# Attention and mixture-of-experts block on one core: new instruction orders for the first three steps and for the routed stage

## What is computed

```python
xn = layernorm(x)
# attention
c  = (xn @ W_to_kv.T) @ W_compress.T                  # 64 values a token
ch = layernorm(c) * gamma + beta
q, k, v = ch @ W_q.T, *split(ch @ W_kv.T)             # q and k get rotary tables
o  = softmax(causal(q @ k.T / 8)) @ v
attn = (o @ W_comp2lat.T) @ (W_to_kv + W_out_res.T) + b_out
# experts
logits = xn @ router_w.T                              # 16 experts, the 2 best are taken
shared = (silu(xn @ sh_gate) * (xn @ sh_up)) @ sh_down
routed = sum over the 2 best e of w_e * (silu(xn @ gate_e) * (xn @ up_e)) @ down_e
out = x + attn + shared + routed
```

## Time and profile before

| | us |
|---|---|
| median of 3 runs (lowest to highest) | 1816.95 (1816.46 to 1821.04) |
| the profiled execution, its own time | 1810.25 |
| its span | 1808.4 |
| PE busy in the span | 1729.9 (96%) |
| DVE, ACT, POOL busy | 1169.6, 751.4, 664.0 |
| prepare, routed, attend, by PE's first matmul of each | 0 to about 690, to 1484, to 1808 |

### The profile page before, as it was taken

The page is one execution under the profiler, slowest core; times in us unless marked ns, Lnnn a source line. Parts: engine busy times, 40 slices in busy tenths (PEclk is TensorE's granted clock), DMA queues, the critical chain, the costliest instruction groups (busy, mean ns, idle before and its releaser), DMA issues. The chain is left out here.

```text
span 1808.4 us, 27930 instructions
## 1 busy us (share of the span) xinstructions
PE 1729.9 (96%) x8349; PEld 1379.7 (76%) x8349; DVE 1169.6 (65%) x2284; ACT 751.4 (42%) x1296; POOL 664.0 (37%) x676
## 2 busy tenths in 40 slices
PE   5699999999999998999999999999999989999998
PEld 3588787787777786788778877778888867777776
DVE  7777677777777663455555555555555537878787
ACT  3232332233223322333333333333333348878885
POOL 2544554445454442333433433433433421111110
PEclk9799999999999999999999999999999999999999
DMA  7767777756777655644544546555444429799896
GB/s 251 247 197 229 244 224 216 254 194 194 209 230 228 209 180 189 206 136 155 181 174 165 175 164 200 181 179 178 159 167 168 175 52 186 196 250 217 213 254 168
DMA packets 149933, 352.50 MB, mean 195 GB/s; under 512 B 20476, under 2 KB 41916, under 8 KB 149824
## 3 DMA queue, kind: packets, MB, share of 16 engines
q1 hardware_dynamic: 97276, 234.52, 39.1%
q0 software_dynamic: 43968, 104.91, 22.6%
q10 hardware_dynamic: 8580, 11.64, 2.3%
HBM read 208.24 MB, written 146.70 MB: 196 GB/s over the span
## 5 line engine op out<-in xcount | busy, mean ns | idle before, releaser
L1488 POOL DMA_INDIRECT expert_rows<-res,ids_all x143 | 149.8, 1048 | 446.3 <-ACT res L1309 437.3
L1429 DVE TENSOR_REDUCE mx<-emb 128x1 f32<-128x512 f32 (+3 forms) x288 | 175.0, 641 | 107.3 <-PE emb L1228 85.9
L70 PE MATMUL egu<-w,rT_0h 128*128 x576 | 186.4, 405 | 0.8 <-DVE rT_0l L1400 0.8
L70 PE MATMUL egu<-w,rT_1h 128*128 x568 | 182.7, 403 | 0.0
L1406 DVE TENSOR_TENSOR eh<-egu,esg 128x256 f32<-128x256 f32 x143 | 60.6, 424 | 182.9 <-ACT esg L1299 182.9
L1035 POOL DMA_INDIRECT token_list<-tok,slot x128 | 126.6, 989 | 116.6 <-DVE slot L741 80.7
L1686 ACT ACTIVATE ex<-sc 128x1024 f32<-128x1024 f32 (+4 forms) x176 | 144.3, 821 | 60.1 <-PE sc L1631 42.7
L1483 POOL DMA_INDIRECT rows<-xn_scratch,rows_all x137 | 132.6, 968 | 48.7 <-issue 43.1
L1299 ACT ACTIVATE esg<-egu 128x256 f32<-128x256 f32 x143 | 55.0, 384 | 202.9 <-PE egu L70 200.2
L1758 POOL DMA_DIRECT2D base<-expert_rows x32 | 41.8, 1538 | 252.2 <-DMA base<-base_scratch 231.4
L1630 PE MATMUL sc<-qh,khl 128*128 128x512 f32 (+3 forms) x288 | 113.1, 393 | 14.4 <-ACT pr_1h L1686 4.5
(11 more groups left out here) (283 smaller groups left out, 4506.1 us busy)
## 6 DMA issues: line engine op xcount, KB each, us to landing
w<-expert_parts SPq DMA_DIRECT2D x64, 768.0 KB, 7.8
base<-expert_rows POOLq DMA_DIRECT2D x32, 1024.0 KB, 12.8
expert_parts<-ew_h SPq DMA_DIRECT2D x32, 768.0 KB, 7.3
expert_parts<-ew_l SPq DMA_DIRECT2D x32, 768.0 KB, 8.5
x<-x SPq DMA_DIRECT2D x16, 1024.0 KB, 6.2
xn_scratch<-xn SPq DMA_DIRECT2D x16, 1024.0 KB, 8.3
base_scratch<-xb SPq DMA_DIRECT2D x16, 1024.0 KB, 11.7
base<-base_scratch SPq DMA_DIRECT2D x16, 1024.0 KB, 11.3
```

The source lines that it names most:

```text
L70: mm = pe.matmul(dst, w, m, start=(first and i == 0), stop=(last and i == len(terms) - 1))
L1429: dve.tensor_reduce(mx[n % 2][:, j, c:c + 1], mb[g % 2][:, 0:width], AX.X, ALU.max).then_inc(m_red, 1)
L1488: pool.indirect_dma_start(parts_d[:, :], bass.IndirectOffsetOnAxis(ap=ids_all[:, t:t + 1], axis=0), res[t % 2][:, :], None, bounds_check=2 ...
```

## The change

In prepare, first():
- ident, w_kv, W_compress and the router come in a list of their own (`first_loads`), on whose semaphore PE, DVE and ACT start; the other small loads come after. The three shared weights are loaded from ACT's queue, gate's into a buffer of its own, so the load of group 1's x no longer waits. The silu table is called for at the start.
- DVE no longer clears `zeros`; POOL does, over xb's second buffer, after the second split. The list is cleared from SP later.

In the first three steps:
- the gate and up products are issued by halves (`shared_half`, 12 matmuls), between the turns. Group 0's blocks f = 0 and 1 and 2 stand in the first step, f = 3 in the second, and the first half of group 1's block 0 goes ahead of the last two turns of group 2 (`third_start`).
- the two halves of experts 0 and 1 move: of the four halves that were split in the first two steps, the high part of the first stays there and its low part goes to the second step, behind the hidden values of f = 2; expert 0's second half goes to the end of the second step; expert 1's two take the places that expert 2's had in the third step, and expert 2's stand behind the second turn of group 3 and at the end of that step.
- POOL takes the roots first; `biased` of group 0 waits for all of group 1's turns (`t_ev`, 8), and that of group 1 stands right behind the root of group 2. Group 0's list is written in two parts in the second step.
- SP's first two steps are written out by hand.

In routed, `turn_hidden` on PE and `hidden_turned` on ACT and DVE go ahead of a tile's third unit of maxima and of the splits; one semaphore is merged into another.

SP's order of the first two steps, and the wait that goes:

```diff
             def load_x(n, q):
-                if known(n, 1):
-                    sp.wait_ge(split_done, 1)
...
+            def first_step():
+                load_cs(1, 1)
+                store_xn(1)
+                clear_list()
+                store_ew(0, 0)
+                load_ew(0, 1)
+                store_qkv(0, 0)
+                load_x(2, 0)
+                store_ew(0, 1)
+                load_ew(1, 0)
+
+            def second_step():
+                load_cs(2, 0)
+                store_xn(2)
+                load_x(3, 1)
+                store_ew(1, 0)
+                load_ew(1, 1)
+                store_qkv(1, 1)
+                store_base(0, 0)
+                store_ew(1, 1)
+                load_ew(2, 0)
```

PE's first step:

```diff
-                pe.wait_ge(consts, CONSTS)
+                pe.wait_ge(first_consts, FIRST_CONSTS)
...
                 shared_gu(0, 0, 0)
+                shared_half(0, 0, 1, 0)
                 turn_c(0)
                 positions(0)
-                shared_gu(0, 0, 1)
+                shared_half(0, 0, 1, 1)
                 qkv(0)
-                for j in range(GT):
-                    turn(1, j)
+                turn(1, 0)
+                turn(1, 1)
+                pe.wait_ge(ht_done, 1)
+                shared_half(0, 0, 2, 0)
+                turn(1, 2)
+                turn(1, 3)
+                shared_half(0, 0, 2, 1)
```

The halves of experts in ACT's third step (DVE's has the same places, with `expert_low`):

```diff
+                late = known(n, 2)
...
-                    expert_high(n, 0)
+                    expert_high(1 if late else n, 0)
...
-                    expert_high(n, 1)
+                    expert_high(1 if late else n, 1)
...
                         turned(n + 1, 1 - q, j)
+                        if late and j == 1:
+                            expert_high(2, 0)
+                if late:
+                    expert_high(2, 1)
```

POOL's second step:

```diff
+            def second_step():
+                root(1, 1, mvc, rsc, mvc_done, rsc_done)
+                listed_rows(0, 0, range(2))
+                root(2, 0, mvx, rsx, mvx_done, rsx_done)
+                biased(0, 1, 1)
+                listed_rows(0, 0, range(2, GT))
+                weighted(1, 1)
```

Routed, on PE and then on ACT (DVE likewise):

```diff
-                for g in maxima(t)[2:]:
-                    max_scores(g, t)
...
                 turn_hidden(t)
+                for g in maxima(t)[2:]:
+                    max_scores(g, t)
```

```diff
+                hidden_turned(t)
                 for n, which in splits[t]:
                     split_high(n, which)
-                hidden_turned(t)
```

More of the change, by code:

```diff
@@ L318, in step @@
             def step(s, n, q):
+                if known(n, 0):
+                    return first_step()
+                if known(n, 1):
+                    return second_step()
                 if n is not None:
@@ L367, in _, with shared_half @@
         def _(pe):
+            def shared_half(s, q, f, i):
+                w = (wgp, wup)[i]
+                if known(s, 0) and f == 0:
+                    pe.wait_ge(split_done, i + 1)
+                mm = parts(pe, gb[2 * (f % 2) + i][:, :], [([a[:, k, f * P:(f + 1) * P] for a in w], [a[:, k, :] for a in xT[q]])
+                                                           for k in range(KD)])
+                if i == 1:
+                    mm.then_inc(f_done, 1)
             def shared_gu(s, q, f):
@@ L375, in shared_gu @@
                     pe.wait_ge(t_ev, 4 * s + 4)
[L376 to L382, removed]
+                for i in range(2):
+                    shared_half(s, q, f, i)
             def shared_down(s, j, ks=(0, FC)):
@@ L485, in second_step, with third_start @@
                 positions(1)
[L486 to L490, removed]
+                shared_down(0, 0, (FC - 1, FC))
+                shared_down(0, 1, (FC - 1, FC))
+                shared_down(0, 2)
+                qkv(1)
+                shared_down(0, 3)
+                turn(2, 0)
+                turn(2, 1)
+            def third_start():
+                pe.wait_ge(d_ev, 2)
+                pe.wait_ge(t_ev, 8)
+                shared_half(1, 1, 0, 0)
+                turn(2, 2)
+                turn(2, 3)
+                shared_half(1, 1, 0, 1)
             def step(s, n, q):
@@ L496, in step @@
                     return second_step()
-                if s is not None:
+                if known(n, 2):
+                    third_start()
+                elif s is not None:
                     shared_gu(s, 1 - q, 0)
@@ L544, in expert_high @@
                 act.wait_ge(ew_in, 96 * n + 48 * c + 48)
+                if known(n, 0) and c == 0:
+                    act.wait_ge(split_done, 1)
                 after(act, ew_st, 64 * n + 32 * c)
@@ L768, in turned_low @@
             def turned_low(n, q, j):
-                if known(n, 1) and j == 0:
-                    dve.wait_ge(cleared, 48)
                 dve.wait_ge(t_hi, 4 * n + j + 1)
@@ L806, in first @@
                 dve.wait_ge(wc_ev, 3)
+                for j in range(GT):
+                    turned_low(0, 0, j)
+                weights_low(0)
+                dve.wait_ge(consts, CONSTS)
+                dve.tensor_copy(before[:, :], tri[:, 0, :])
+                dve.tensor_copy(carry[:, :], rt[:, GT, :])
                 dve.tensor_copy(wqkp[0][:, :], wqk[:, :]).then_inc(wqk_ev, 1)
@@ L1021, in step, with listed_rows @@
                     return
-                if not known(n, NG - 1) and not known(n, 0):
+                if known(n, 0):
+                    return first_step()
+                if known(n, 1):
+                    return second_step()
+                if not known(n, NG - 1):
                     root(n + 1, 0, mvx, rsx, mvx_done, rsx_done)
                 root(n, 1, mvc, rsc, mvc_done, rsc_done)
-                if known(n, 0):
-                    root(1, 0, mvx, rsx, mvx_done, rsx_done)
+                if known(n, 2):
+                    listed_rows(1, 1)
                 weighted(n, q)
                 biased(s, n, q)
+                listed_rows(n, q)
+            def listed_rows(n, q, blocks=range(GT)):
                 pool.wait_ge(slot_done, n + 1)
@@ L1032, in step @@
                 hold(pool, pool_gate)
-                for j in range(GT):
+                for j in blocks:
                     for c in range(2):
```

175 lines of the change are left out of this document (98 added, 77 removed).

## The result

The changed kernel takes 1813.23 us (median of 22 runs, 1808.78 to 1818.54) and the kernel before, beside it, 1817.85: a ratio of 0.9972, 95% interval 0.9962 to 0.9981, so 5.1 us faster.

A forecast was written before the change was run, and what follows sets the result against it. PE was taken as the bound, busy 1729.9 of 1808.4 us, leaving 78 us idle to win. Prepare's 2 us plus routed's 4.5 made 6.5, taken from the 1816.95 median: 1810.5 us, range 1799 to 1822.

The forecast's parts named there:

- The start: Prepare up to group 1's logits: first gate product at 24.7, logits at 46 instead of 66.65, 20.6 us won.
- Second step: Prepare: group 2's xn at 75.5, a new PE wait of 7 us, group 1's first gate product at 76.
- The rule of the Trainium skill: Group 2's normalization: VectorE and GpSimd exclude each other per instruction, first issuer holding the ports; 2.8 us better if VectorE led.
- Third step: Prepare: logits begin 18 us early; expert 1's second half is split at about 109.
- Fourth step: Prepare: f = 3 begins at about 151, PE waits 7 to 8 us again, 2 us stay won in prepare.
- three trips of 10: Third to fourth step: one buffer's round trips, 10 us each, put expert 3's first low part at 146.5 to 148.3.
- the halves cost more than the start gives: Rival, prepare: trips of 13.9 us put f = 3 at 160, total 1822.5; decided at about 12.5 a trip; chance 0.16.
- the one for "wrong": Signs against the forecast: groups 3's and 4's steps without PE waits, or prepare ending later than 690.
- The clock's fall: Prepare: after idle time PE restarts at the lower clock, estimated at 3 us each time.
- From there on the steps are the old ones with no idle time: Prepare after the fourth step: steps as before without PE idle time, the shift carried to the end.
- Routed: Routed stage: splits no longer stand before the hidden values' copy; 4.5 us won, bounds 0 and 5.9.
- a third unit of maxima stood ahead of the turn without harm: Routed, 30 tiles: the third unit of maxima ahead of the turn was taken to cost nothing.

The follow-up runs named there:

- combined kernel: Changed kernel with experts' halves one behind throughout prepare, POOL's group 1 bias before group 2's root, group 3's x loaded before expert 0's second-half store: 1800.79 us, ratio 0.9884.
- the late half: From the third step, a step's second expert half behind f = 3's hidden values: on before 1810.37 us, on the changed kernel 1805.56, on the combined kernel 1788.20.

## Why the prediction came out near, and what in it was wrong

**The start: right.** First gate product forecast at 24.7, measured 24.68; group 1's logits 46 and 45.83; 20.6 us won and 20.8.

**Second step: right.** Group 2's xn 75.5 and a wait of 7; PE went on at 76.92 after 8.04. Group 1's first gate product came at 78.54, not 76: two turns stand ahead of it (1.6 us), which I had not counted. The normalization beside the bias took 5.59 us, where I had counted 4.7. It is the alternation of the earlier trace rows, once more: each of its four instructions took 1.39 to 1.48 us beside an add of 1.26 to 1.44, where before only three did and the fourth, behind the last add, took 0.53. The rule of the Trainium skill (SBUF — State Buffer, Who interferes with whom) that I set beside it gave 2.8 us better if VectorE went first; here the trace has it first nowhere: POOL's adds began at 71.12, the normalization at 71.28, and it ended 0.3 us behind them.

**Third step: one wait missed.** I had no term for group 3's x. SP issued it at 84.05, behind the store of expert 0's second half, which hangs on group 2's normalization, and DVE had it 11.7 us later, where the earlier trace rows has 6.2. That costs PE 3.67 us at 104.29, and puts expert 1's second half at 113.11 instead of 109.

**Fourth step: the step that failed.** It was "three trips of 10". From the end of a low part to the start of the next it was 13.6, 13.7 and 11.7 us, 39.0 instead of 32, and with the 4.1 us above expert 3's first low part came at 157.43 instead of 146.5. I had taken 9.9 us a trip from one row, and three of those are 29.8. Of the 9.3 us above that, 6.9 lie between the store's issue and ACT's high part (9.8, 12.1 and 10.1 us, where the row of before took 8.4), almost all of it in the wait for the load to land; 2.3 are DVE's, in the first trip alone, where roping, sums and slots stood ahead of the low part. In the second and third trip DVE stood idle and took the half at once, so it was the transfer that held them. Before's own trace had such trips, with x issued ahead and the stores of q, k and v behind; this one takes 14.7 us from store to high part:

```profile
134.72 0.44 SPq L311 DMA_DIRECT2D expert_parts<-ew_h  x1
```

```profile
149.38 1.48 ACT L546 CAST ew_h<-ew 128x1536 fp32r<-128x1536 f32 x1 [2.13 <-DMA ew<-down_w]
```

So f = 3 began at 161.67, not 151, and 11.9 us were waited in two places, not 7 to 8 in one. That the catch-up as such is the cause is shown by the kernel that spreads it, where of these two waits one is gone and the other is 2.6 us; why the loads took longer to land is open. This is the mechanism of the rival "the halves cost more than the start gives", whose bound of about 12.5 us a trip was passed by the mean of the three (13.0). I had it at 0.16, and 10 us dear; it cost less (2.9 us against before by time). Of my own signs, the one for "wrong", a prepare that ends later than 690, came true too: the last product of prepare ended at 704.0 instead of 690.4, and PE's first egu moved from 697.0 to 709.6. The clock's fall was over-rated each time and counted too seldom: behind the wait at 104.29 (granted clock 0.72 from 104 to 110) ten matmuls take 3.97 us where ten at the higher level take 2.3, so 1.7 us and not 3, and the same count gives 1.9, 2.4 and 2.1 behind the waits at 76.92, 147.50 and 161.67. That is some 8 us in four places, where I had 6 in two.

**"From there on the steps are the old ones with no idle time": wrong for both kernels.** The profile of before that I read was one of the two calm ones of four: 440.6 us for eleven steps, where others took 448 and 450, and 435.7 are enough. That changes no term of the difference, since both kernels leak alike, but it is likely why the two spans by themselves have the wrong sign, and it is where the larger gain lay.

**Routed: direction right, less than half the size.** The splits gave 5.4 us by tiles (4.8 when moved alone) and 6.9 by time, over the 4.5 I took and around the upper bound of 5.9. The term that was missing is the one I wrote off with "a third unit of maxima stood ahead of the turn without harm": no wait, but 0.11 us in each of 30 tiles once the splits are out of the way.

So the forecast of 6.5 us came out near by luck: it holds two misses of 5 us, one each way.

## What to carry to other kernels

When work is put off out of a start that is too slow, cost its catch-up by the whole cycle of the resource it shares (here low part, store, load, high part, and the place in each engine's list), and compare it with spreading the lag over all later steps: that alone was worth some 10 us. In engines that run in order, a step that waits for a transfer belongs behind the steps whose results others await; look for it where executions of one kernel differ, since a wait of 1 to 2 us that comes and goes costs every step and may be absent from the one profile at hand. And no wait is not no cost: read the spacing of the instructions too.

## What was not expected of the hardware

In the combined kernel, one 64x512 subtraction on DVE, 0.69 us elsewhere, took 5.79 us beside POOL's bias:

```profile
62.49 5.79 DVE L796 TENSOR_TENSOR chs<-t,chs 64x512 fp32r<-64x512 f32 x1
```

```profile
62.74 4.98 POOL L1082 TENSOR_TENSOR xb<-x,bias 128x512 f32<-128x512 f32 x4
```

It stood until all four of POOL's adds were through, though by the profile it began 0.25 us ahead of the first of them; the adds ran in 4.98 us instead of the 6.81 of the earlier trace rows. In the kernel with the bias alone brought forward, and in the combined one with the late half, the subtraction took 5.78. In the earlier trace rows the split of a half began within 0.01 us of the same adds and lost only 1.1 us. Which of the two happens I can't say from these runs; where POOL adds over two operands in memory, a DVE instruction with two such operands must be costed up to the whole group, not one add of it. That wait is the 2.90 us that the bias brought forward costs PE in return.

**Open.** By the profiles, prepare of after ends 6 us later than that of before (first egu, means of three and of four), by time it costs 2.9 us with an interval from 0.9 to 4.9; so few profiles, with a scatter of 13 us, don't settle it. With the late second half the eleven steps no longer scatter (435.7 and 435.1 us), and there after is 4.7 us behind before at the fifth step and 3.1 at the first egu (698.7 against 695.6), by one profile each. Where a step's first half waits for nothing, PE still waited 0.9 us now and then for the low part of the hidden values; the late second half removes that too, and I have not shown how. A second buffer for the halves was not tried.
